# Attention output merged by 4 strided DMAs, reciprocals spread in 4 KB pieces, a third plane loaded by two DMAs

## The reference, cut to what matters

```
q = heads(x @ Wq); k = heads(ctx @ Wk); v = heads(ctx @ Wv)     # 20 heads of 16 channels
o = softmax(q @ k.T / 4) @ v                                    # per batch and head, 77 keys
x = merge(o) @ Wo + bias + x
```

## Time and profile before

| | |
|---|---|
| median of 3 runs | 929.96 us (929.67 to 931.31) |
| span of the profiled execution | 926.1 us; the median of the runs is 3.9 us above it |
| TensorE busy | 903.4 us, 98% |
| VectorE / ScalarE / GpSimd busy | 685.7 / 544.6 / 402.8 us |
| weight loads busy (they overlap matmuls) | 681.3 us |
| DMA moved | 112.41 MB, mean 121 GB/s |

### The profile page before, as it was taken

The page is one execution under the profiler, slowest core; times in us unless marked ns, Lnnn a source line. Parts: engine busy times, 40 slices in busy tenths (PEclk is TensorE's granted clock), DMA queues, the critical chain, the costliest instruction groups (busy, mean ns, idle before and its releaser), DMA issues.

```text
span 926.1 us, 28090 instructions
## 1 busy us (share of the span) xinstructions
PE 903.4 (98%) x11518; PEld 681.3 (74%) x11518; DVE 685.7 (74%) x1221; ACT 544.6 (59%) x549; POOL 402.8 (43%) x229
## 2 busy tenths in 40 slices
PE   8899999999999999999999999999999999999897
PEld 5777778777787777777777777777778777777665
DVE  3775787868778686787868688786786868678557
ACT  4456565656556556666556656556665656656553
POOL 3424263633436263366624446364344625433224
PEclk9999999999999999999999999999999999999999
DMA  6313534445444544545555444544534544443342
GB/s 203 102 32 80 138 93 132 135 124 148 98 119 119 164 131 110 149 115 140 141 148 140 102 118 113 137 132 123 134 95 118 139 131 134 102 130 78 86 134 94
DMA packets 80526, 112.41 MB, mean 121 GB/s; under 512 B 21200, under 2 KB 37878, under 8 KB 80400
## 3 DMA queue, kind: packets, MB, share of 16 engines
q1 hardware_dynamic: 80208, 110.35, 44.4%
q10 hardware_dynamic: 192, 0.26, 0.2%
HBM read 60.24 MB, written 22.24 MB: 89 GB/s over the span
## 4 chain that ended last, share of the span: by engine, by line
PE 82%; DVE 6%; DMA 4%; SPq 3%; issue 2%; ACT 1%; POOL 1%; DVEq 0%; ACTq 0%; POOLq 0%
PE pR L307 27%; PE pR L444 14%; PE pA L391 10%; PE pR L378 8%; PE pR L287 4%; PE pR L329 4%; PE pR L257 4%; DMA X<-in_xT 2%; PE pA L397 2%; PE pR L261 2%; DVE OS L1090 2%; SPq L1434 1%; PE pA L307 1%; DVE QL L995 1%; PE pR L244 1%
## 5 line engine op out<-in xcount | busy, mean ns | idle before, releaser
L763 ACT ACTIVATE P<-pA 77x2048 f32<-77x2048 f32 x160 | 300.4, 1878 | 197.2 <-PE pA L397 196.9
L1034 DVE TENSOR_REDUCE Mx<-pR 128x4 f32<-128x308 f32 (+1 forms) x480 | 259.2, 575 | 31.8 <-PE pR L378 26.6
L1293 POOL TENSOR_TENSOR On<-On,OS 128x1024 f32<-128x1024 f32 (+1 forms) x58 | 105.8, 1845 | 257.8 <-DMA OS<-rd 257.8
L307 PE MATMUL pR<-OS,Wo 128*128 128x512 f32 x638 | 168.1, 402 | 2.9 <-DVE OS L1090 2.1
L444 PE MATMUL pR<-P,VA 77*17 77x256 f32 x2480 | 157.4, 385 | 0.8 <-ACT P L763 0.5
L378 PEld LDWEIGHTS pR<-KH,QH 32*128 32x128 f32 x1280 | 96.3, 183 | 70.8 <-issue 46.6
L391 PE MATMUL pA<-QH,KH 32*77 32x256 f32 x1280 | 145.0, 291 | 0.1
L1258 POOL TENSOR_TENSOR XS<-X,XS 128x1024 fp32r<-128x1024 f32 x31 | 74.0, 2387 | 152.1 <-ACT XS L649 152.1
L378 PE MATMUL pR<-KH,QH 32*128 32x154 f32 x1280 | 131.5, 283 | 7.8 <-DVE X L1101 2.2
L307 PEld LDWEIGHTS pR<-OS,Wo 128*128 128x128 f32 x638 | 113.8, 188 | 33.2 <-issue 6.3
L391 PE MATMUL pA<-QL,KH 32*77 32x256 f32 x1280 | 134.9, 275 | 0.0
(11 more groups left out here) (161 smaller groups left out, 1289.6 us busy)
## 6 DMA issues: line engine op xcount, KB each, us to landing
On<-Oraw SPq DMA_DIRECT2D x244, 64.0 KB, 2.7
OS<-rd SPq DMA_DIRECT2D x58, 256.0 KB
C<-in_cT SPq DMA_DIRECT2D x16, 616.0 KB, 7.9
X<-in_xT SPq DMA_DIRECT2D x16, 512.0 KB
y<-X SPq DMA_DIRECT2D x16, 512.0 KB, 4.0
X<-y SPq DMA_DIRECT2D x16, 512.0 KB
out<-X SPq DMA_DIRECT2D x15, 512.0 KB, 4.0
X<-in_xT SPq DMA_DIRECT2D x16, 256.0 KB
```

The costliest lines, as they stand in the source:

```text
L307: f = pe.matmul(p[:, :], W[:, k, c0:c0 + 128], S[:, s, :], start=(i == 0), stop=(i == len(pairs) - 1))
L763: act.activation(P[0:L, i % PR, :, :], pA[0:L, :, :], ACT.Exp, scale=float(D) ** -0.5).then_inc(p_done, 1)
L1034: dve.tensor_reduce(Mx[:, :, :].rearrange("p t (j i) -> p j t i", j=4)[:, j:j + banks, :, i:i + 2], pR[:, bank:bank + banks, 0:2 * LK].rea ...
L1293: pool.tensor_tensor(On[rows, blocks, :], On[rows, blocks, :], recips(u, part).bitcast(F32), ALU.mult).then_inc(o_mul, 1)
```

## The change

1. Values lie in VA as [10 ones, 320 values, 10 ones], the heads in an order HPOS in which a head of even number and the one after it are 10 places apart. A PV matmul takes 32 columns, 10 apart. For an even head its values fall on even columns, for an odd one on odd columns, with the ones on column 31 or 0; the other columns are another head's and aren't read. So an output block has its values in even or in odd rows and its sum in row 31 or 0.
2. `Oraw` holds groups 0, 2, 1, 3, 4 in this order, so that `natural` moves all even rows of groups 0 and 2 by one DMA of 64 partitions x 4 KB, all odd rows of groups 1 and 3 by another, and the last 64 channels by two DMAs: 4, not 12. The rows of Wo are reordered on the host to match.
3. `sums` of groups 0 and 2, and of 1 and 3, are one DMA each, the last group's are two. Those of groups 0 and 2 of an even chunk are fetched in the next step.
4. `spread` of part 0 has for each parity 4 source rows of 4 KB, each repeated over 16 partitions (before: for each block 8 rows of 2 KB); with the last 64 channels' DMA these are 3, as before.
5. The third plane of x comes by two DMAs of 64 partitions.
6. `V_last` makes six copies for each tile in place of two.

```diff
-        VA = sb("VA", [128, 2, 2, C + H])
+        VA = sb("VA", [128, 2, 2, HH + C + HH])
...
+            def columns(t, first, step):
+
+                return bass.AP(t.tensor, t.offset + first, [list(t.ap[0]), [step, 32]])
...
+                g = HPOS[h]
+                return columns(VA[0:L, u % 2, b, :], HH + g if g >= HH else g, HH)
...
-                        f = pe.matmul(bank[32 * j:32 * j + D + 1, b * SQ:b * SQ + SQ], VA[0:L, u % 2, b, h:C + H:H], src,
+                        f = pe.matmul(bank[32 * j:32 * j + 32, b * SQ:b * SQ + SQ], values_and_one(u, b, h), src,
...
-                act.wait_ge(d_x[x], 32 * (u // XR + 1))
+                act.wait_ge(d_x[x], 48 * (u // XR + 1))
...
+                for h in range(16, H):
+                    g = HPOS[h]
+                    act.activation(halves[:, h % 2, :, g:g + 1], v[:, :, g:g + 1], ACT.Copy)
                 for p in range(2):
...
+                    heads = slice(HPOS[p], HPOS[p] + 8)
+                    f = act.activation(striped[:, :, p, heads], v[:, :, heads], ACT.Copy)
...
-                act.activation(Oraw[:, k, :], psum(slot["PV", u, k])[:, :], ACT.Copy).then_inc(o_raw[k][u % 2], 1)
+                act.activation(Oraw[:, OSLOT[k], :], psum(slot["PV", u, k])[:, :], ACT.Copy).then_inc(o_raw[k][u % 2], 1)
...
-                sp.dma_start(X32[:, x, 2, :],
-                             src[256:C, cols].rearrange("(h p) n -> h p n", h=1).broadcast_to([2, 64, N])).then_inc(d_x[x], 16)
+                for half in range(2):
+                    sp.dma_start(X32[64 * half:64 * half + 64, x, 2, :], src[256:C, cols]).then_inc(d_x[x], 16)
...
-                    for j in range(4):
-                        sp.dma_start(On[32 * j + D * r:32 * j + D * r + D, 0:2, :],
-                                     Oraw[32 * j:32 * j + D, r:r + 3:2, :]).then_inc(d_on[r], 16)
+                    sp.dma_start(On[(EVEN, ODD)[r], 0:2, :], Oraw[(EVEN, ODD)[r], 2 * r:2 * r + 2, :]).then_inc(d_on[r], 16)
...
-                for j in range(4):
-                    sp.dma_start(On[D * j:D * j + D, 2, :], Oraw[32 * j:32 * j + D, 4, :]).then_inc(d_ont, 16)
+                sp.dma_start(On[0:32, 2, :], Oraw[0:64:2, 4, :]).then_inc(d_ont, 16)
+                sp.dma_start(On[32:64, 2, :], Oraw[65:128:2, 4, :]).then_inc(d_ont, 16)
...
-                for m in ((0, 1), (2,))[part]:
-                    src = a["rd"][u, 8 * m * N:min(8 * m + 8, H) * N].rearrange("(h o c) -> h o c", o=1, c=N)
-                    sp.dma_start(recips(u, part)[:, m % 2, :].bitcast(F32),
-                                 src.broadcast_to([MT[m] // D, D, N])).then_inc((d_rb, d_rbt)[part], 16)
+                if part == 0:
+                    for p in range(2):
+                        src = a["rd"][u, 8 * p * N:8 * p * N + 8 * N].rearrange("(j o c) -> j o c", o=1, c=2 * N)
+                        sp.dma_start(recips(u, part)[(EVEN, ODD)[p], :, :].rearrange("p m n -> p (m n)").bitcast(F32),
+                                     src.broadcast_to([4, D, 2 * N])).then_inc(d_rb, 16)
+                    return
+                src = a["rd"][u, 16 * N:H * N].rearrange("(h o c) -> h o c", o=1, c=N)
+                sp.dma_start(recips(u, part)[:, 0, :].bitcast(F32), src.broadcast_to([4, D, N])).then_inc(d_rbt, 16)
...
-                    sums(u, 0)
                     load_x(u + 3)
                 else:
                     sums(v, 2)
+                    sums(v, 0)
                     sums(v, 1)
```

More of the change, by code:

```diff
@@ L30 @@
 QC = 2 * N + SQ
+OSLOT = (0, 2, 1, 3, 4)
+HH = H // 2
+HPOS = [HH * (1 - h % 2) + h // 2 for h in range(16)] + [18, 19, 8, 9]
 WORDER = ["Wk0", "Wq0", "Wv0", "Wo0", "Wk1", "Wv1", "Wq1", "Wo1"]
@@ L96, in build @@
         mask = sb("mask", [128, 2])
-        small = sb("small", [128, 4 * D])
-        ones = small[0:L, :].rearrange("p (a d) -> p a d", a=2)
-        Zt = small[96:128, :]
+        small = sb("small", [128, 34 + 3 * D])
+        stripes, blocks = small[0:L, 0:34], small[0:L, 34:34 + 3 * D]
+        Zt = small[96:128, 0:4 * D]
         bias = sb("bias", [128, 2, 3])
@@ L174, in last_o @@
             return OL[:, m, :] if m < 2 else OL2[:, :]
+        EVEN, ODD = slice(0, 128, 2), slice(1, 128, 2)
         count = {}
@@ L471, in PV_last @@
                                 first = half == 0
-                            f = pe.matmul(dst, VL[0:L, b, h:2 * C:H] if what == "OL" else ones[:, pp, :], src,
+                            g, vl = HPOS[h], VL[0:L, b, :]
+                            if what == "ZL":
+                                lhs = stripes[:, pp:pp + 32] if m < 2 else blocks[:, D * pp:D * pp + 32]
+                            else:
+                                lhs = columns(vl, g, H)
+                            f = pe.matmul(dst, lhs, src,
                                           start=first, stop=True, skip_group_check=True)
@@ L1300, in split_o @@
                 pool.tensor_tensor(OS[:, 3:5, :], On[:, 0:2, :], OS[:, 0:2, :].bitcast(F32), ALU.subtract).then_inc(o_lo, 1)
-            pool.memset(VA[:, :, :, C:C + H].rearrange("p a b c -> p (a b) c"), 1.0)
+            for c in (0, HH + C):
+                pool.memset(VA[:, :, :, c:c + HH].rearrange("p a b c -> p (a b) c"), 1.0)
             pool.memset(CS[:, :, L4:L4 + 12].bitcast(F32), 0.0)
             for p in range(2):
-                pool.memset(ones[:, p, D * p:D * p + D], 1.0)
-                pool.memset(ones[:, p, D - D * p:2 * D - D * p], 0.0)
+                pool.memset(stripes[:, p:34:2], 1.0 - p)
+            for i in range(3):
+                pool.memset(blocks[:, D * i:D * i + D], 1.0 - i % 2)
             pool.memset(Mx[:, :, :], 0.0).then_inc(pads, 1)
@@ L1400, in values @@
                         if u < NU - 1:
-                            src, dst = VS[row:row + rows, t, :], VA[done:done + rows, half, b, 0:C]
+                            src, dst = VS[row:row + rows, t, :], VA[done:done + rows, half, b, HH:HH + C]
                         else:
@@ L1405, in values, with sums @@
                         done += rows
-            def sums(u, m):
+            def sums(u, r):
                 if u < 0:
                     return
-                z = Oraw[D:128:32, :, :].rearrange("p q c -> p (q c)")
-                for k in range(2 * m, min(2 * m + 2, NG)):
+                for k in ((0, 2), (1, 3), (4,))[r]:
                     sp.wait_ge(o_raw[k][u % 2], u // 2 + 1)
-                if m < 2:
+                if r < 2:
                     if u:
                         sp.wait_ge(d_rw, 16 * u)
-                    sp.dma_start(Zg[64 * m:64 * m + 64, :],
-                                 z[:, 2 * m * N:(2 * m + 2) * N].rearrange("p (i c) -> p i c", c=64)).then_inc(d_zg, 16)
+                    z = Oraw[31 * (1 - r):128:32, 2 * r:2 * r + 2, :].rearrange("p q c -> p (q c)")
+                    sp.dma_start(Zg[64 * r:64 * r + 64, :], z.rearrange("p (i c) -> p i c", c=64)).then_inc(d_zg, 16)
                 else:
@@ L1421, in sums @@
                         sp.wait_ge(d_rwt, 16 * u)
-                    sp.dma_start(Zt[:, :], z[:, 4 * N:5 * N].rearrange("p (i c) -> p i c", c=64)).then_inc(d_zt, 16)
+                    for i, row in enumerate((31, 64)):
+                        sp.dma_start(Zt[16 * i:16 * i + 16, :],
+                                     Oraw[row:row + 33:32, 4, :].rearrange("p (i c) -> p i c", c=64)).then_inc(d_zt, 16)
             def natural(u, r):
@@ L1594 @@
     ident, mask, neg = constants()
+    pairs = np.arange(C).reshape(C // 32, 2, D).transpose(0, 2, 1).reshape(C)
+    rows = np.concatenate([pairs[0:256], np.arange(256, C)])
     w = {k: np.asarray(v) for k, v in inputs.items()}
@@ L1601 @@
         "Wv0": by_d(w["L0_xattn_to_v_w"]),
-        "Wo0": dup(w["L0_xattn_to_out_w"]),
+        "Wo0": dup(w["L0_xattn_to_out_w"][rows]),
         "Wq1": dup(w["L1_xattn_Wq"].T),
```

36 lines of the change are left out of this document (18 added, 18 removed).

## The result

The changed kernel takes **959.46 us** (median of 4 runs, 951.14 to 960.73) against 930.16 us for the kernel before on the same chip: 1.0291 of it, 95% interval 1.0255 to 1.0327. The forecast was 937.8 with a range to 952. The sign was right, the size was not; rival C's 959.3 is what came, but not by C's sum, as the experiments show.

What follows compares the result with a forecast made beforehand. The prediction took TensorE (PE), busy 98% of the span, to bound the kernel. Its terms, -1.4-0.7+3.1+0+4.2+2.6=+7.8 us on a median of 929.96, gave 937.8 us, range 928 to 952.

Steps and rivals of the forecast that it cites:

- rival C: T=10 passes its limit in each even chunk: 21.7 us there, 6.6 in the tail; 959.3 us; chance 0.15.
- Reciprocals spread by pieces of 4 KB: Even chunks: half the outer rows per DMA raise T to 8.4 us, and PE waits for the excess; +4.2 us.
- T: Time from the reciprocal spread's first issue to GpSimd's multiply; predicted 8.4 us, PE waiting beyond 8.3 in even chunks.
- chain from the rounding to the copies at 619.94: Even chunk: delay passes from ScalarE's rounding through differences to VectorE's copies, which free PE's bank; 0.15 us of room.
- PV with 32 columns: PV's weight loads take 138 ns, not 109, open 108 times where PE starts a call; +3.1 us.
- Merge by 4 DMAs: SyncE saves eight issues per chunk, 5.3 us, but no period's chain waits for it: 0 there, counted in the tail.
- Third plane: Two DMAs over 64 rows land x's third plane earlier: -1.4 us at the start, -0.7 in the middle.
- The tail: End of the kernel: spread at 855 +1.1, value copies +0.7, last spread +0.8; together +2.6 us.

Runs made afterwards that it cites:

- a_gap: The kernel after, with GpSimd's low part of the attention output in even steps waiting for VectorE's subtraction: 936.48 us, 1.0061 of the kernel before.
- b_cols: The kernel before with 32 weight columns in PV, 10 floats apart, in place of 17 (other values wrong): 933.2 us, 1.0026.
- a_best: a_twice with V laid out by pairs of heads, so that PV's 32 weight columns lie side by side: 925.06 us, 0.9943.
- a_merge8: a_twice with each merge of 64 rows cut into four DMAs of 16, ten merge DMAs in a chunk, not four: 932.0 us, 1.0022.
- a_twice: The kernel after with the reciprocals written to DRAM twice, so that each spread has eight source rows, pieces still 4 KB: 927.61 us, 0.9969.
- b_four: The kernel before with its reciprocals spread by four DMAs of four source rows, not two of eight, pieces still 2 KB: 1004.65 us, 1.0797.
- a_four: The kernel after with the reciprocals written four times, so that each spread reads 16 source rows: 930.39 us, 0.9993.

## Why the prediction was wrong in size

**The step that failed** is "Reciprocals spread by pieces of 4 KB", its term +4.2. It failed in two places.

1. T was taken at 8.4 and is 8.95 us in the mean of the even chunks. The row from which it was scaled (160 KB in 9.97 us, so 128 KB in 8.0) was a load without a queue of other spreads and stores around it; whether that made the difference no run shows. By the prediction's own rule, all of an even chunk's excess over 8.3 less 0.15 of room, that gives 14 x (8.95-8.3-0.15)=7.0 us in place of 4.2: a miss of 3 us, inside the range. The prediction named a rule of the Trainium skill (page "DMA: Bandwidth & Descriptors", section "Why a DMA increments its semaphore by 16 and not by 1"), by which the slowest dimension sets how many queues work. The traces bear out its direction with 4, 8 and 16 rows (8.95, 6.5, 4.6 us), with less than a doubling in time for each halving of rows.
2. The rule itself, one microsecond late is one microsecond lost, was wrong. The spread's part of the change is 1.0291-0.9969, 30 us. Of these, a_gap takes back 1.0291-1.0061, 21 us, with T unchanged; 1.0061-0.9969, 9 us, are left for the lateness as such, the holds that remain and whatever the late store costs, in the periods and in the tail, against the 6.1 that the prediction had for both. The 21 us are what the hold on VectorE's subtraction and QL<-Qt adds once the multiply is late: PE's waits behind them, and the lower clock that follows a wait.

The mechanism was there to be read before. In the kernel before, GpSimd stood for 0.1 to 2.6 us between its multiply and its low part in every even step (0.92 us in the step at 108 us), because ScalarE's rounding came behind the softmax. The late multiply filled that pause: in 12 of the 14 even steps of the kernel after GpSimd runs on (the row at 115.98 has 8.56 us of idle time ahead of the multiply and the next row none), and the multiply itself now lies over QH<-Qt, which had mostly been done beside its end or behind it. In ten of the 14 even steps that cast takes 1.7 to 2.5 us, as here, where 0.29 would do:

```profile
174.60 2.37 DVE L1013 CAST QH<-Qt 128x256 fp32r<-128x256 f32 x1
```

The subtraction is another case, since it had been held all along. Before, it started 12.7 us after the spread's issue in the mean and ended at 15.0, in time for the copies. After, it starts at 14.4; undisturbed it would end at 15.1 (an estimate, 14.4 and 0.69), but it ends at 16.4. In a_gap it starts at 14.1 and the copies at 14.8. So the kernel before could pay for the hold and the lateness took what it paid with: PE waits for the sum of the two. The prediction's chain from the rounding to the copies at 619.94 has the hold in it, as a fixed part, and its rule of one for one has no place for the holds of 3.3 us and more that the late multiply brings. The median of L1090, 1448 ns for an operation that takes 684, was the warning.

**Rival C** gave the right time for a wrong reason: T=10 in every even chunk at one for one. T was never above 9.4 there.

**PV with 32 columns.** +3.1 predicted; +2.4 by b_cols, and 2.4 back in a_best, each inside an interval of about 2 us to either side; loads at 138 ns as said. Right, as far as this resolves it.

**Merge by 4 DMAs.** 0 predicted in the periods, and in the tail 0.9 and 1.2 us for two issues that come earlier; -4.9 and -5.9 measured for six of the eight DMAs less. The prediction argued that no chain runs over SyncE's merges in a period, and there it was right: from 110 to 165 us PE works 54.94 of 55.00 us in a_merge8 and in a_twice. Outside the periods the merges were worth more than its 2.1 us. Two rows place a part of it, the stretch from 520 us, around the border of the two layers, in a_merge8 and in a_twice:

```profile
520.00:560.00 40.00, 38.93 (x449) 30.37 (x446) 30.24 (x56) 24.76 (x27) 15.64 (x9) 1.00 0.47 136
```

```profile
520.00:560.00 40.00, 39.87 (x474) 31.48 (x465) 30.32 (x57) 25.57 (x28) 15.67 (x10) 1.00 0.45 137
```

That is 0.9 us; from 560 to 620 us it is 59.25 us of work against 59.93, and from 880 us on the mean granted clock is 0.93 against 0.99. Why the tail has the lower clock is not shown. In b_four, with twelve merges and two more issues for the spread, late sums reached PE; that SyncE's slack is cover for such lateness fits this, but is not shown by itself.

**Third plane.** -2.1 predicted. The start moved as said (12.09); measured alone it was +1.2 us with an interval of 2.3 to either side, and -3.8 in a_twice. Not settled.

**The tail** (+2.6) was not measured by itself; its spread part is within the 9 us above, and V_last's instructions were not tried.

The parts add up: spread +30, columns +2.4, merges -5.4, plane between -3.8 and +1.2 give +23 to +28; measured +27.

## What to carry to other kernels

A transfer that repeats few source rows into many partitions was the faster here the more source rows it had (4, 8, 16): writing the small source twice, 32 KB more, took 2.4 us off the spread in even chunks and 1.9 in odd ones, and was worth 30 us in all. When a transfer that was hidden gets later, don't price it microsecond for microsecond; look at what its consumer does behind it without a pause, and at which short operations of another engine it will then lie over. An operation whose median is twice its shortest duration in the profile is already being held, and is harmless only as long as there is room ahead of it. And one wait that orders two engines can be worth more than the work that it delays.

## What the hardware showed that I had not expected

VectorE operations with both inputs in SBUF can stand while GpSimd works, and can stand for more than one GpSimd instruction. 64x512 takes 1.4 to 2.4 us in place of 0.69 beside one, and 3.33 over two; KL<-Kt, 0.37 alone, 2.5 beside the multiply in a_four; QL<-Qt, 0.41 alone, took 4.46 over three and, in b_four, 7.32 over five. The cast QH<-Qt, from SBUF to SBUF, is held too: 0.29 us in one chunk, 2.03 in another. The rows show the end 0.3 to 0.6 us behind the end of a GpSimd instruction: 307.68 behind 307.12, 693.23 behind 692.95. Copies and maxima from PSUM beside the same GpSimd work kept their durations. The Trainium skill, page "SBUF — State Buffer", section "Who interferes with whom", says that a VectorE instruction with two SBUF inputs and a GpSimd instruction that reads SBUF exclude each other, and that the one that issues second waits until the first is done. The trace agrees on who excludes whom; it differs in the length, for at 688.77 VectorE did not get its turn at 689.47, when GpSimd's instruction ended and the next one began, nor at 691.80. Here VectorE went through only where GpSimd itself stood, for 0.08 us ahead of 693.03. Elsewhere it got in between two GpSimd instructions that follow each other without a pause: QL<-Qt at 177.59 in the kernel after takes 0.80 us, across their border at 178.1. What decides the turn between two GpSimd instructions these runs don't show.
